# ScalarE's order in the start-up: router exponentials before up's first high half, gate's second high half behind the third Silu

## The reference

```python
x = x + xattn(layernorm(x), ctx, ctx)          # single head, softmax over 120 context rows
h = layernorm(x)
probs = softmax(h @ router_w.T)                # 8 experts
a_h = gelu(h @ actor_w1.T + actor_b1)          # 50 wide
logits = clip(a_h @ actor_w2.T + actor_b2, -30, 30)
k = argmax(logits) + 1                         # how many experts this token takes (1 to 6)
scores = where(rank(probs) < k, probs, 0)
out = sum_e scores[e] * (silu(h @ gate_w[e].T) * (h @ up_w[e].T)) @ down_w[e].T
x = x + out                                    # hidden size 336 for each expert
```

## Time and profile before

| what | us |
|---|---|
| median of 3 runs (751.5 to 751.68) | 751.64 |
| the profiled execution | 751.69 |
| its span | 749.9 |

### The profile page before, as it was taken

The page is one execution under the profiler, slowest core; times in us unless marked ns, Lnnn a source line. Parts: engine busy times, 40 slices in busy tenths (PEclk is TensorE's granted clock), DMA queues, the critical chain, the costliest instruction groups (busy, mean ns, idle before and its releaser), DMA issues.

```text
span 749.9 us, 13834 instructions
## 1 busy us (share of the span) xinstructions
PE 739.5 (99%) x3721; PEld 365.6 (49%) x3721; DVE 628.9 (84%) x1395; ACT 552.5 (74%) x978; POOL 578.9 (77%) x620
## 2 busy tenths in 40 slices
PE   8999999999999999999999999999999999999998
PEld 5544454544445445454544545445454544544445
DVE  7899888897888788788888888888888887978777
ACT  5998787776877776777766777776777767777664
POOL 2687979789796887969689696886968688687763
DMA  9200312304032132312323132132323312120110
GB/s 352 69 17 1 83 31 56 59 14 97 24 78 56 49 79 55 84 41 69 70 40 93 38 84 62 41 84 54 77 48 69 72 28 56 31 59 11 28 30 29
DMA packets 107271, 45.40 MB, mean 61 GB/s; under 512 B 86872, under 2 KB 97112, under 8 KB 107224
## 3 DMA queue, kind: packets, MB, share of 16 engines
q1 hardware_dynamic: 106792, 44.39, 24.5%
q10 hardware_dynamic: 432, 0.48, 0.2%
HBM read 26.46 MB, written 10.78 MB: 50 GB/s over the span
## 4 chain that ended last, share of the span: by engine, by line
PE 91%; ACT 3%; DVE 3%; issue 1%; POOL 1%; DMA 0%; DVEq 0%; ACTq 0%; POOLq 0%
PE bank L633 28%; PE bank L635 28%; PE bank L634 28%; PE bank L543 2%; PE bank L516 2%; PE bank L629 1%; PE bank L527 1%; PE bank L592 1%; PE bank L611 1%; ACT silu L971 0%; DMA x_in<-in_x 0%; POOL weighted L1206 0%; DVE bank L1561 0%; ACT up_hi L828 0%; ACT L1007 0%
## 5 line engine op out<-in xcount | busy, mean ns | idle before, releaser
L1206 POOL TENSOR_TENSOR weighted<-silu,score_bc 128x512 f32<-128x512 f32 x336 | 431.6, 1299 | 90.3 <-ACT silu L971 88.1
L1561 DVE SCALAR_TENSOR_TENSOR bank<-bank,h_scale,weighted 128x512 f32<-128x512 f32 x336 | 253.6, 755 | 94.6 <-PE bank L635 76.4
L965 ACT ACTIVATE hid_hi<-bank 128x512 f16<-128x512 f32 x336 | 200.8, 598 | 156.1 <-DVE bank L1561 155.4
L971 ACT ACTIVATE silu<-bank,silu_scale 128x512 f32<-128x512 f32 x336 | 230.5, 686 | 24.4 <-PE bank L635 24.2
L1567 DVE TENSOR_TENSOR hid_lo<-bank,hid_hi 128x512 f16<-128x512 f32 x336 | 227.9, 678 | 0.1
L633 PE MATMUL bank<-xn_lo,gate_hi 128*128 128x512 f16 x336 | 127.5, 380 | 1.3 <-ACT silu L971 1.3
L633 PE MATMUL bank<-xn_lo,up_hi 128*128 128x512 f16 x336 | 127.4, 379 | 1.2 <-DVE hid_lo L1567 1.1
L635 PE MATMUL bank<-xn_hi,up_hi 128*128 128x512 f16 x336 | 127.3, 379 | 0.0
L634 PE MATMUL bank<-xn_hi,up_lo 128*128 128x512 f16 x336 | 127.3, 379 | 0.0
L635 PE MATMUL bank<-xn_hi,gate_hi 128*128 128x512 f16 x336 | 127.3, 379 | 0.0
L634 PE MATMUL bank<-xn_hi,gate_lo 128*128 128x512 f16 x336 | 127.3, 379 | 0.0
(11 more groups left out here) (200 smaller groups left out, 778.3 us busy)
## 6 DMA issues: line engine op xcount, KB each, us to landing
x_in<-in_x SPq DMA_DIRECT2D x16, 256.0 KB, 2.8
y_kept<-y_sb SPq DMA_DIRECT2D x60, 64.0 KB, 2.6
y_tok<-y_kept SPq DMA_DIRECT2D x15, 256.0 KB, 2.8
out<-out_sb SPq DMA_DIRECT2D x15, 256.0 KB, 2.1
xt_in<-in_x_t SPq DMA_DIRECT2D x14, 256.0 KB, 2.9
row_bc<-row_kept SPq DMA_DIRECT2D x14, 256.0 KB, 3.5
ctx_in<-in_ctx_t SPq DMA_DIRECT2D x14, 240.0 KB, 2.8
p_kept<-y_sb SPq DMA_DIRECT2D x10, 256.0 KB, 2.0
```

Of the source, the lines that this page charges most:

```text
L965: af(hid_hi[j % HRING][:], up_bank[j % U_BANKS][:], ACT.Copy).then_inc(hid_hi_ready, 1)
L971: af(silu[j % RING][:], gate_bank[(par + j) % G_BANKS][:], ACT.Silu, scale=silu_scale[:])\
L1206: g.tensor_tensor(weighted[j % RING][:], silu[j % RING][:], score_bc[par][:], ALU.mult)\
L1561: v.scalar_tensor_tensor(up_bank[j % U_BANKS][:], up_bank[j % U_BANKS][:], h_scale[:], weighted[j % RING][:], ALU.mult, ALU.mult).then_inc ...
```

## The change

In ScalarE's start-up list, `weight_high(1)` moves from ahead of `router_exps(0)` to behind `turned_probs(1)`, where `weight_high(2)` stood; `weight_high(2)` moves behind `gated(0, 0, 2)`, ahead of `values(4)`. Nothing is added or left out.

```diff
             tanh(0)
             keys(4, up_bank[0])
             exps(1)
-            weight_high(1)
             router_exps(0)
             nc.scalar.preload_act_table(ACT.Silu)
             gated(0, 0, 0)
             turned_probs(1, up_bank[1])
-            weight_high(2)
+            weight_high(1)
             score_copy(0)
             gated(0, 0, 1)
             score_spread(0, 0)
             weight_sums(8)
             gated(0, 0, 2)
+            weight_high(2)
             values(4, up_bank[2])
             turns(act, turn)
```

## The result

The changed kernel takes 753.27 us (median of 13 runs, 753.15 to 753.63) against 751.56 us before in the same series (13 runs, 751.47 to 753.07, all but one below 751.7). The ratio is 1.0022, with an interval of 1.0015 to 1.003. It is 1.7 us slower, where 1.2 was forecast, just over the line of 0.2% and 0.07 us over the upper end of the range. The profiled execution took 753.35, with a span of 751.4.

What follows compares the result with a forecast made beforehand. PE's fixed work bounds the kernel from about 65 us; before that, each us PE gets its work later counts at the end. Terms: -0.25 + 0.25 (gain lost again) + 0.49 + 0.70 = +1.2, giving 752.8 us; range 751.3 to 753.2.

Steps and rivals of the forecast that it cites:

- Term 1: Up to 34 us: without `up_hi` ahead, the router's exponentials and the score path come earlier, -0.25 us.
- Term 2: ScalarE's values' copy stands behind `gate_hi`, so PE's third up waits for the bank: +0.49 us.
- Term 3: VectorE's `gate_lo` at 40.21 meets GpSimd's multiply of tile 5, already running, and takes 2.05 us: +0.70 us.
- Rivals 1 and 2: VectorE is first at `gate_lo`'s meeting, +0.3 (chance 0.25); the third up's bank wait doesn't bind, 751.4 (chance 0.12).
- Rival 3: `up_lo` at 46.78 loses a second meeting with GpSimd, paying 0.9 and not 0.3: +1.8, 753.4; chance 0.10.
- the forecast's own bound: `gate_lo` costs at most 1.15 + 1.10, paying the full overlap with GpSimd's multiply: sum +1.4.

Runs made afterwards that it cites:

- the first experiment: Changed kernel with `values(4)` ahead of `weight_high(2)` on ScalarE: 751.22 us, ratio to before 0.9994.
- both edits: Changed kernel with `w_top` made from a PSUM column and one SBUF operand, and `gate_lo` behind `hidden(0, 3)` and `low(0, 2)`: 752.14 us, ratio 1.0006.
- the third experiment: Changed kernel with `w_top` made from a PSUM column and one SBUF operand, tensor_tensor in place of tensor_scalar: 752.77 us, ratio 1.0014.
- the second part alone: Kernel before with only `weight_high(2)` moved, behind the third Silu and ahead of `values(4)`; `up_hi` left ahead of the router's exponentials: 753.55 us, ratio 1.0028.
- the fourth experiment: Changed kernel with `weight_low(2)` (`gate_lo`) behind `hidden(0, 3)` and `low(0, 2)` on VectorE: 752.74 us, ratio 1.0014.

## Why the prediction was wrong

- **Term 1** (-0.25, the router earlier): right. 0.27 at the exponentials, 0.26 at the third Silu, and 0.23 at the end of the start-up in the kernel that keeps it (the first experiment).
- **Term 2** (+0.49 at the third up): right. 0.48 at the third up, 0.50 at `w_top_col`. Its worth at the end no run shows by itself: the 0.51 of both edits holds it and two terms of about 0.2 that cancel.
- **Term 3** (+0.70, gate_lo behind a multiply): right in kind and size. `gate_lo` took 2.00 in place of 1.34, +0.66; in the third experiment 2.07 and a sum of +1.19. Rivals 1 and 2 did not come about. But its place was not the forecast one: see below.
- **The step that failed** is the sentence that what is queued behind `w_top_col`, "the tile 2, the scales, `gate_lo`", is 0.49 late. It carried `w_top` over at its old 0.22 us. I had looked for meetings with GpSimd only among the low halves, the long instructions, and let a 2x2 one pass because it is tiny. It met the multiply of tile 3 at 37.62 and took 0.83: a missing term of 0.61. With it the parts are 0.48 + 0.61 + 0.66 = 1.75, where 1.78 was measured. The prediction's own numbers had it: `w_top` 0.49 late is at 37.83, the multiply 0.25 early runs from 37.37 to 38.64, and the rest of 0.81 less 0.2 is 0.61.
- **A second step failed with it**, that the sixth Silu "hardly moves". In the third experiment that holds, and `gate_lo` and the multiply stand 14.33 and 14.18 behind `route_less`, close to the forecast 14.35 and 14.18. In the changed kernel the `hid_hi` ahead of that Silu waits for VectorE (0.45 us of idle time at 39.15), the Silu is 0.55 late relative, and the two stand at 14.98 and 14.75: both sides of the meeting moved by about 0.6, so it kept its price. Had the multiply stayed at 14.18, `gate_lo` would have met its last 0.47 only and taken about 1.4 (an estimate by the same price), and the sum would have been near +1.2 even with `w_top`'s term.
- **Rival 3** had the right kind, a second lost meeting of 0.6, and a time near the measured one (753.4). Its place and its condition were wrong: it was looked for at 46.78, where `up_lo` took 1.43 before and 1.41 after. The place that decided is the one at which PE's wait lets GpSimd get ahead of VectorE. That its time came close is luck. The chance of 0.10 for a second lost meeting was too low, and the range, 0.07 us short, took in the forecast's own bound but no second meeting.
- **The assumption that nothing behind 45 us gives back or adds** held within 0.02 us: relative lateness at the first down and at the last wait is 1.77 and 1.78 in the changed kernel, 2.01 and 2.01 with the second part alone, 1.19 and 1.19 with `w_top` made from PSUM, -0.24 and -0.23 with the copy first.

## What to carry to other kernels

Before a long instruction is put ahead of a copy that empties a PSUM bank, look for who fills that bank next: here the copy had 0.24 us of slack against PE, and got 0.93 of work in front of it. When two engines that hold each other up, as VectorE and GpSimd do here, are shifted against each other, walk through every instruction of the later one in its new place, the tiny ones too, and see what runs on the other engine at that moment; a 2x2 instruction can wait by the same measure as a 128x896 one. Look at both sides of a meeting: a delay can move the other engine's instruction with it. A shift of half a microsecond was here worth 1.78.

## What the runs showed of the hardware

Where `gate_lo` (128x896) or `w_top` (2x2, SBUF to SBUF) starts while GpSimd's multiply is running, it gets longer by the rest of the multiply less about 0.2 us. For `gate_lo`, whose undisturbed length is 1.15:

| kernel | rest of the GpSimd instruction, us | longer by, us |
|---|---|---|
| before | 0.40 | 0.19 |
| `gate_lo` behind tile 3, on the first experiment | 0.60 | 0.40 |
| changed kernel | 1.05 | 0.85 |
| `w_top` made from PSUM | 1.12 | 0.92 |

`w_top` fits too. The two multiplies in the row at 37.17 last 2.50 together, so the first ends at about 38.42, 0.80 behind `w_top`'s start, and `w_top` was 0.61 longer; with the second part alone it took 0.81 and in the fourth experiment 0.82. VectorE's own multiply by up (L1561, in the third experiment's kernel L1562), which reads one tensor from PSUM and one from SBUF, is not held up: in the third experiment it started at 37.71 beside the same GpSimd multiply and took 0.76, against 0.74 in the changed kernel. Where the constant 0.2 comes from no run shows.
